# Reordering the start-up of a two-layer attention and mixture-of-experts kernel: which loads and clears stand ahead of the first slots

## The reference, cut to what matters

```python
x = x + tanh(g_xattn[0]) * attention(layernorm(x), ctx; 16 heads of 8, Wq Wk Wv Wo with biases)
x = x + tanh(g_ffn[0])   * experts(layernorm(x); 8 experts, hidden 256, each expert claims its best 512 tokens)
x = x + tanh(g_xattn[1]) * attention(layernorm(x), ctx; 16 heads of 8, no biases, no output matrix)
x = x + tanh(g_ffn[1])   * experts(layernorm(x); 8 experts, hidden 512, the best 2 of each token)
```

## Time and profile before

| | |
|---|---|
| runs (3) | 758.35, 759.71, 764.55 us; median 759.71 us |
| the profiled execution | 760.45 us, of which the trace spans 758.6 us |
| busy share of the span | PE 71%, PEld 57%, DVE 66%, ACT 47%, POOL 42% |
| chain that ended last | PE 41%, DVE 22%, issue 11%, POOL 10%, DMA 8%, ACT 5% |
| mean granted clock of PE | 0.869 |

### The profile page before, as it was taken

How to read it: one execution, slowest core, us unless ns; L and a number is a source line. 1 busy time by engine, 2 the same in 40 slices (tenths; PEclk the granted TensorE clock), 3 DMA queues, 4 the chain that set the end, 5 groups by cost and what they waited for, 6 DMA issues and landing times.

```text
span 758.6 us, 16969 instructions
## 1 busy us (share of the span) xinstructions
PE 539.6 (71%) x5534; PEld 435.7 (57%) x5534; DVE 502.7 (66%) x1605; ACT 358.3 (47%) x830; POOL 315.0 (42%) x439
## 2 busy tenths in 40 slices
PE   0699999998721039872699988888403999999940
PEld 0466777776510028761466756665302999999940
DVE  5568888887358862222699999998561556655625
ACT  0246777776633014330167766677402555555510
POOL 6212222221200057743755227456772455555440
PEclk9959999999955558996599999999755999999985
DMA  8443334332000004362556546241123222222229
GB/s 262 153 136 92 101 109 115 107 88 66 16 14 1 0 21 97 99 84 66 146 163 185 163 135 190 84 121 53 40 64 101 61 69 71 79 72 72 65 70 296
DMA packets 100532, 74.50 MB, mean 98 GB/s; under 512 B 12928, under 2 KB 94592, under 8 KB 100160
## 3 DMA queue, kind: packets, MB, share of 16 engines
q1 hardware_dynamic: 92336, 55.17, 25.5%
q0 software_dynamic: 7040, 14.56, 7.6%
q10 hardware_dynamic: 1072, 3.70, 1.4%
HBM read 43.64 MB, written 31.39 MB: 99 GB/s over the span
## 4 chain that ended last, share of the span: by engine, by line
PE 41%; DVE 22%; issue 11%; POOL 10%; DMA 8%; ACT 5%; SPq 2%; ACTq 1%; POOLq 0%; DVEq 0%
PE bank L943 10%; PE bank L953 10%; DVE MX L1089 7%; PE bank L740 5%; POOL PT L582 5%; PE bank L766 4%; PE bank L887 4%; PE bank L754 3%; POOL dispatched L556 3%; DVE PT L1285 2%; DMA PT<-normed,LIST 2%; PE bank L842 1%; ACT XT_HL_WR L654 1%; DMA QS_N<-MH 1%; ACT OT L678 1%
## 5 line engine op out<-in xcount | busy, mean ns | idle before, releaser
L623 ACT ACTIVATE PT<-bank 128x512 f32<-128x512 f32 x256 | 151.8, 597 | 95.1 <-PE bank L754 93.9
L1089 DVE TENSOR_REDUCE MX<-bank 128x4 f32<-128x512 f32 x256 | 172.1, 681 | 25.9 <-PE bank L766 24.2
L766 PE MATMUL bank<-KS,QS_N 96*128 96x128 f16 x1024 | 104.5, 228 | 16.7 <-DVE MX L1089 8.7
L593 POOL DMA_INDIRECT returned<-PT,META_ROW x78 | 74.9, 961 | 84.6 <-DVE PT L1403 72.4
L953 PEld LDWEIGHTS bank<-WALL,HT 128*128 128x128 f32 x808 | 100.9, 194 | 5.1 <-issue 1.7
L953 PE MATMUL bank<-WALL,HT 128*128 x808 | 102.1, 278 | 0.6 <-issue 0.6
L943 PE MATMUL bank<-XGT,XT_HL_WR 128*128 128x256 f32 x404 | 101.9, 392 | 0.0
L766 PEld LDWEIGHTS bank<-KS,QS_N 96*128 96x128 f16 x1024 | 76.6, 103 | 43.4 <-DVE MX L1089 15.3
L754 PE MATMUL bank<-QS_N,KS 98*128 98x512 f16 x256 | 98.0, 388 | 1.8 <-DMA QS_N<-MH 1.6
L943 PEld LDWEIGHTS bank<-XGT,XT_HL_WR 128*128 128x128 f32 x404 | 75.0, 198 | 8.0
L556 POOL DMA_INDIRECT dispatched<-N,SLOT x64 | 64.3, 1004 | 30.0 <-issue 14.1
(11 more groups left out here) (210 smaller groups left out, 917.4 us busy)
## 6 DMA issues: line engine op xcount, KB each, us to landing
spread<-XT_HL_WR SPq DMA_DIRECT2D x96, 128.0 KB, 2.0
QS_N<-spread SPq DMA_DIRECT2D x128, 48.0 KB
KS<-spread SPq DMA_DIRECT2D x32, 192.0 KB
PT<-dispatched SPq DMA_DIRECT2D x39, 132.0 KB, 2.1
WALL<-in_w SPq DMA_DIRECT2D x8, 578.0 KB
CT<-in_ctx SPq DMA_DIRECT2D x32, 128.0 KB
returned<-PT SPq DMA_DIRECT2D x23, 128.0 KB, 2.2
WALL<-in_w ACTq DMA_DIRECT2D x1, 2048.0 KB, 8.5
```

What stands on the lines that cost most here:

```text
L593: pool.indirect_dma_start(ys[1][:, :], bass.IndirectOffsetOnAxis(ap=META_ROW[:, a.f, c:c + 1], axis=0), YS[:, a.f, c, :], None).then_inc(S ...
L623: nc.scalar.activation(PT[:, c, 4 * g:4 * g + 4, :].rearrange("p j q -> p (j q)"), ST[i % 2][:, :], ACT.Exp, scale=SCALE[layer]).then_inc( ...
L766: last = nc.tensor.matmul(MB[i % 2][:, j * P:(j + 1) * P], QS[0:96, m.r, J * g + j, c * P:(c + 1) * P], KS[0:96, m.r, g, c * P:(c + 1) * P ...
L1089: V.tensor_reduce(out=MX[:, m.u, 2 * J * g + c:2 * J * (g + 1):2], in_=MB[i % 2][:, :].rearrange("p (j k) -> p j k", j=J), op=ALU.max, axi ...
```

## The change

SP loads the first two batches of `x` ahead of everything, on a semaphore of their own, then only four loads on `loaded`: the identity columns of `CONST`, `WSQ` 0 to 3, `VEC` and `GATES`. The other six of the first eight batches and three rest loads (the other columns of `CONST`, `WG`, `WSQ` 4 to 6) are issued by SP at slot -3, ahead of the context of pair 1. ACT takes the tanh at once, issues the other 24 batches at slot -2 and `ROWS` and `WALL` at slot 1. POOL clears `EXPO` and one quarter of `QS` first, and the others at the entry of slots -3 and -2; `KS` and the last quarter at slot -1. Each entry waits for POOL's own bias addition of the slot before. DVE clears one quarter of `VA` at the entry of each of the slots -4 to -1, makes `BIAS` at slot -3 ahead of the statistics of pair 1, three small clears at slot 1, and the four casts when the expert layer begins. The waits are moved to match.

```diff
-        LOADS = 6
+        LOADS, REST = 4, 3
...
         @block.sync
         def _(sp):
-            loads = [(CONST[:, :], const_in),
-                     (X[:, 0:FIRST * D].rearrange("p (b d) -> p b d", b=FIRST), x_in[0:FIRST].rearrange("b p d -> p b d")),
-                     (WSQ[:, :, :], wsq_in), (GATES[:, :], gates_in), (WG[:, :, :], wg_in), (VEC[:, :], vec_in)]
+            load_x(0, 2, x_first)
+            loads = [(CONST[:, 0:P], const_in[:, 0:P]), (WSQ[:, 0:4, :], wsq_in[:, 0:4, :]), (VEC[:, :], vec_in), (GATES[:, :], gates_in)]
...
+            def rest_of_loads(p):
+                if p == -3:
+                    load_x(2, FIRST, x_second)
+                    rest = [(CONST[:, P:], const_in[:, P:]), (WG[:, :, :], wg_in), (WSQ[:, 4:7, :], wsq_in[:, 4:7, :])]
+                    for to, of in rest:
+                        sp.dma_start(to, of).then_inc(rest_loaded, 16)
+                padding(p)
...
-                    sp.wait_ge(set_pool, 6)
+                    if r.g < 4:
+                        sp.wait_ge(set_pool, (2, 3, 4, 6)[r.r])
...
-            nc.gpsimd.memset(KS[96:98, :, :, :], SHIFT).then_inc(set_pool, 1)
+            def queries(r):
+                nc.gpsimd.memset(QS_N2[0:96, 2 * r * H * P:2 * (r + 1) * H * P].bitcast(F32), 0.0).then_inc(set_pool, 1)
+            nc.gpsimd.memset(EXPO[:, :], -0.5).then_inc(set_pool, 1)
             pool.wait_ge(set_pool, 1)
+            queries(0)
             pool.wait_ge(set_pool, 2)
-            for r in range(4):
-                nc.gpsimd.memset(QS_N2[0:96, 2 * r * H * P:2 * (r + 1) * H * P].bitcast(F32), 0.0).then_inc(set_pool, 1)
-                pool.wait_ge(set_pool, r + 3)
-            pool.wait_ge(loaded, 16 * LOADS)
+            def clear(p):
+                if p in (-3, -2, -1):
+                    pool.wait_ge(x_bias, p + 4)
+                if p in (-3, -2):
+                    queries(p + 4)
+                    pool.wait_ge(set_pool, p + 6)
+                if p == -1:
+                    nc.gpsimd.memset(KS[96:98, :, :, :], SHIFT).then_inc(set_pool, 1)
+                    pool.wait_ge(set_pool, 5)
+                    queries(3)
+                    pool.wait_ge(set_pool, 6)
...
             act.wait_ge(loaded, 16 * LOADS)
-            act.dma_start(X[:, FIRST * D:].rearrange("p (b d) -> p b d", b=B - FIRST),
-                          x_in[FIRST:].rearrange("b p d -> p b d")).then_inc(x_loaded, 16)
-            act.dma_start(ROWS[:, :], rows_in).then_inc(experts_loaded, 16)
-            act.dma_start(WALL[:, 0:E * WCOLS[0]], w0_in).then_inc(experts_loaded, 16)
             nc.scalar.activation(GATES[:, :], GATES[:, :], ACT.Tanh).then_inc(act_own, 1)
+            def rest_of_loads(p):
+                if p == -2:
+                    act.dma_start(X[:, FIRST * D:].rearrange("p (b d) -> p b d", b=B - FIRST),
+                                  x_in[FIRST:].rearrange("b p d -> p b d")).then_inc(x_loaded, 16)
+                if p == 1:
+                    act.dma_start(ROWS[:, :], rows_in).then_inc(experts_loaded, 16)
+                    act.dma_start(WALL[:, 0:E * WCOLS[0]], w0_in).then_inc(experts_loaded, 16)
...
             pe.wait_ge(loaded, 16 * LOADS)
-            pe.wait_ge(set_dve, 8)
...
+            def set_up(p):
+                if p < 0:
+                    r = p + 4
+                    V.memset(VA[:, r, :, :, :], 0.0).then_inc(set_dve, 1)
+                    dve.wait_ge(set_dve, 2 * r + 1)
+                    heads = VA[:, r, :, :, :].rearrange("p c h w -> p (c h w)").rearrange("p (k e w) -> p k e w", e=4, w=2 * HD)
+                    V.memset(heads[:, :, 0:4:3, HD:HD + 1], 1.0).then_inc(set_dve, 1)
+                    dve.wait_ge(set_dve, 2 * r + 2)
+                if p == -4:
+                    dve.wait_ge(x_first, 16)
+                if p == -3:
+                    dve.wait_ge(loaded, 16 * LOADS)
+                    dve.wait_ge(act_own, 1)
+                    dve.wait_ge(bias_done, 1)
+                    link(V.tensor_tensor(out=VEC[:, 0:D], in0=PO[:, 0:D], in1=VEC[:, 0:D], op=ALU.add))
+                    V.tensor_scalar(out=BIAS[:, :], in0=VEC[:, 0:D], scalar1=GATES[:, 0:1], scalar2=None,
+                                    op0=ALU.mult).then_inc(bias_done, 1)
+                    dve.wait_ge(x_second, 16)
+                if p == 0:
+                    dve.wait_ge(x_loaded, 16)
+                if p == 1:
+                    V.memset(MASKG[:, 0, 0, :], 0.0).then_inc(set_dve, 1)
+                    V.memset(N[:, :, D:ROW], 0.0).then_inc(set_dve, 1)
+                    V.memset(RX[:, 0:1], 0.0).then_inc(set_dve, 1)
+                    dve.wait_ge(set_dve, 11)
+                    dve.wait_ge(rest_loaded, 16 * REST)
...
             def expert_layer(layer):
                 if layer == 0:
+                    casts()
                     probabilities(layer)
```

More of the change, by code:

```diff
@@ L382, in _, with load_x @@
         def _(sp):
[L383 to L386 removed]
+            def load_x(b0, b1, sem):
+                sp.dma_start(X[:, b0 * D:b1 * D].rearrange("p (b d) -> p b d", b=b1 - b0), x_in[b0:b1].rearrange("b p d -> p b d")).then_inc(sem, 16)
+            load_x(0, 2, x_first)
+            loads = [(CONST[:, 0:P], const_in[:, 0:P]), (WSQ[:, 0:4, :], wsq_in[:, 0:4, :]), (VEC[:, :], vec_in), (GATES[:, :], gates_in)]
+            assert len(loads) == LOADS and at["ident"] == (0, P)
             for to, of in loads:
                 sp.dma_start(to, of).then_inc(loaded, 16)
+            def rest_of_loads(p):
+                if p == -3:
+                    load_x(2, FIRST, x_second)
+                    rest = [(CONST[:, P:], const_in[:, P:]), (WG[:, :, :], wg_in), (WSQ[:, 4:7, :], wsq_in[:, 4:7, :])]
+                    assert len(rest) == REST
+                    for to, of in rest:
+                        sp.dma_start(to, of).then_inc(rest_loaded, 16)
+                padding(p)
             def padding(p):
@@ L476, in second_experts @@
                     sp.dma_start(N2[:, b, 0:D], y[:, b, :]).then_inc(YL[k], 16)
-            pair_slots(0, attention_slot, padding)
+            pair_slots(0, attention_slot, rest_of_loads)
             first_experts()
@@ L594, in second_experts @@
                                                 YS[:, a.f, c, :], None).then_inc(SC[a.f], 16)
-            pair_slots(0, attention_slot(0))
+            pair_slots(0, attention_slot(0), clear)
             first_experts()
@@ L727, in _ @@
             for layer in range(2):
-                pair_slots(layer, attention_slot(layer))
+                pair_slots(layer, attention_slot(layer), None if layer else rest_of_loads)
                 expert_layer(layer)
@@ L969, in _ @@
             link = chain.link
[L970 to L974, removed]
-            V.tensor_copy(BEFORE[:, :], const("before")).then_inc(set_dve, 1)
-            V.tensor_copy(ONES[:, :], const("ones")).then_inc(set_dve, 1)
@@ L977, in _ @@
-            V.tensor_copy(SAME[:, :], const("same_expert")).then_inc(set_dve, 1)
-            V.tensor_copy(SHARE[:, :], const("region_share")).then_inc(set_dve, 1)
-            V.memset(MASKG[:, 0, 0, :], 0.0).then_inc(set_dve, 1)
-            V.memset(N[:, :, D:ROW], 0.0).then_inc(set_dve, 1)
-            V.memset(RX[:, 0:1], 0.0).then_inc(set_dve, 1)
-            dve.wait_ge(set_dve, 9)
-            dve.wait_ge(act_own, 1)
-            dve.wait_ge(bias_done, 1)
-            link(V.tensor_tensor(out=VEC[:, 0:D], in0=PO[:, 0:D], in1=VEC[:, 0:D], op=ALU.add))
@@ L986, in _ @@
-            V.tensor_scalar(out=BIAS[:, :], in0=VEC[:, 0:D], scalar1=GATES[:, 0:1], scalar2=None,
-                            op0=ALU.mult).then_inc(bias_done, 1)
+            def set_up(p):
[24 more added lines that the diff above has]
+                    dve.wait_ge(rest_loaded, 16 * REST)
@@ L989, in stats, with casts @@
+            def casts():
+                V.tensor_copy(BEFORE[:, :], const("before")).then_inc(set_dve, 1)
+                V.tensor_copy(ONES[:, :], const("ones")).then_inc(set_dve, 1)
+                V.tensor_copy(SAME[:, :], const("same_expert")).then_inc(set_dve, 1)
+                V.tensor_copy(SHARE[:, :], const("region_share")).then_inc(set_dve, 1)
+                dve.wait_ge(set_dve, 15)
             def stats(pair, tmp, mv):
```

18 lines of the change are left out of this document (11 added, 7 removed).

## The result

The changed kernel takes 756.0 us (median of 20, 752.43 to 762.29) against 759.49 us (median of 20): ratio 0.9959, 95% interval 0.9942 to 0.9975, so 1.9 to 4.4 us faster. The prediction was 751.7, 8.0 us faster. The sign and the place were right, the size was more than double. 756.0 lies inside the range, 748.7 to 756.5, but outside the forecast's own, 750.5 to 754. The profiled execution after took 754.38 us, of which the trace spans 752.5; only three of the 20 were quicker, so the 6.1 us between the two spans overstate the change's effect.

A forecast was written before the change was run, and what follows sets the result against it. The prediction took a serial start (loads, ACT's issues and tanh, `VEC`) as the bound. 9.8 - 1.3 - 0.5 = 8.0 us off 760.45 gave 752.45, with the median 0.74 lower 751.7; range 748.7 to 756.5, forecast's own 750.5 to 754.

The forecast's parts named there:

- S: Moment pair 0's last read-back lands and slot -1 begins: 29.37 us before, 20.9 predicted, 8.5 early.
- ACT: At the start, ACT's three DMA issues leave, so the tanh is done at 6.7 us instead of 15.1.
- Casts: Four casts move to where DVE idles 5.07 us for the last logits; bounds 0 and 2.1 us, 0 taken.
- DVE's start, slot -3: Transposes at 6.1 us, not 18.48; low part ends at 12.9, not 22.67, with POOL's 1.85 clear on the path; 9.8 remain.
- Transfers beside it: ACT's 24 batches run beside the third write and first reads; bounds 0 and 5.0 us lost, 1.3 taken.
- Slot -1, slot 0: POOL's chain ends at 23.1 us, wanted at 24.1, so hidden; slot 0 unchanged, padding still ahead of `MH`.
- Slot 1: `ROWS` and `WALL` load beside pair 1's `MH`; bounds 0 and 3.9 us lost, 0.5 taken.
- The second rule: All engines' DMAs interleave on the same 16 DMA engines; taken strictly, the sum is 4.3 us, or 755.4.
- B: Rival: POOL or the queues bound the start, with contention and late `GATES`; 5.1 us early, 754.6; chance 0.14.
- C: Rival: in slot 1 `WALL` delays `MH` to slot start + 9.0 and keeps PE's clock down; slower, 762.5; chance 0.04.
- A: Rival: no contention and PE's clock rises sooner; at best 10.9 us early, 748.8, centre 750; chance 0.16.
- D: Rival: the reordering doesn't reach S, as six batches or pair 0's context land late; 757; chance 0.04.

The follow-up runs named there:

- clears_twice: pieces_late with the second quarter of `QS` cleared three times over at slot -3; 754.37 us against 760.73 for the kernel before, ratio 0.9910.
- clears_later_alone: The changed kernel with each of POOL's clears one slot later, loads as they are; 758.29 us against 761.0 for the kernel before, ratio 0.9958.
- clears_later: pieces_late with each of POOL's clears one slot later; 748.75 us against 760.73 for the kernel before, ratio 0.9839.
- tables_late: The changed kernel with `ROWS` and `WALL` issued at slot 16 instead of slot 1; 795.77 us against 801.98 for the kernel before, ratio 0.9925.
- x_in_pieces: The changed kernel with the 24 batches loaded in six pieces of four, two slots ahead of use; 795.14 us against 801.98 before, ratio 0.9917.
- pieces_late: The changed kernel with both load edits, those of x_in_pieces and tables_late; 751.02 us against 760.73 for the kernel before, ratio 0.9858.
- again: The changed kernel unaltered, run once more; 797.49 us against 801.98 for the kernel before on the same chip, ratio 0.9948.
- after: The changed kernel in its first measurement and trace; 756.0 us against 759.49 for the kernel before, ratio 0.9959.
- again_2: The changed kernel unaltered, for a third trace; 757.61 us against 761.0 for the kernel before, ratio 0.9961.
- padding_late: clears_later with SP's 1 MB of padding issued at slot 16 instead of slot 0; 748.43 us against 761.0 for the kernel before, ratio 0.9831.
- before_again: The kernel before, unaltered, for a second trace; 760.21 us against 761.0 for the kernel before, ratio 0.9994.
- before_tanh_first: The kernel before with one edit, ACT's tanh ahead of its three DMA issues; 759.44 us against 760.73 for the kernel before, ratio 0.9987.
- clear_in_gap: The changed kernel with POOL's clear of the second quarter of `QS` moved from slot -3 into slot -4; 797.4 us against 801.98 before, ratio 0.9951.

## Why the prediction was right or wrong

- **What bounds the start.** Right: serial, loads then ACT then `VEC`. clears_twice shows that S moves the whole, one for one.
- **Loads.** Right: 128 KB of `x` land 2.1 us after issue (2.3 taken), `GATES` at 5.3 (5.2).
- **ACT.** Right in effect. The tanh ended at 5.50 and not 6.7, since the table load now stands ahead of the wait, at 0.74. It bought little: DVE's clear of `VA` ran until 6.80, and `VEC` and `BIAS` ended at 7.45, 7.5 having been said.
- **Casts.** Right, 0 in the sum: 0.16 to 0.22 us each behind, in front of an idle time of 4.77 us. The lines of the grouped view of DVE after, 200 to 213 us, with the row that answers to the earlier trace rows:

```profile
L1038 DVE CAST SAME<-CONST 128x128 bf16<-128x128 f32 x1 | 0.2, 219 | 0.0
```

```profile
211.84 0.42 DVE L1241 TENSOR_REDUCE SM<-LG 128x32 f32<-128x256 f32 x1 [4.77 <-ACT LG L716]
```

- **DVE's start, slot -3.** Right: transposes at 5.91 (6.1), low part ended at 12.64 (12.9) behind pair 1's `XN`, POOL's clear at 8.31 in front of it. That this clear is worth 1.85 us was right only for a kernel whose write isn't held: 0 in clears_later_alone, 1.3 at S in clears_later.
- **Transfers beside it: the step that failed first.** I took 1.3 us out of bounds of 0 and 5.0. The third write took 5.04 instead of 1.94, 3.1 more. The size was off because the mechanism was: I took half of one queue's delay because "here it is two", and two queues were no relief. The load's packets went first for 2 us, then one for one with the writes' smaller ones. Net of a low part 0.3 us early and shorter reads, S came 7.3 us early in the mean of the traces and not 8.5.
- **Slot -1, slot 0.** POOL's chain ended at 22.7 and was hidden, as said. Slot 0 had its padding wait, 3.71 us. But slot -1 lasted 9.09 us in all three traces of the changed kernel, and 8.35 and 8.85 before. The sum had no term for that. In tables_late, where PE took half as long for its queries, it lasted 8.15.
- **Slot 1: the step that failed second.** I took 0.5 us out of bounds of 0 and 3.9; `MH` took 6.32 us and landed with the large load: 40.95 + 8.5 = 49.45, and 43.47 + 6.32 = 49.79. It cost 1.1 us in the slot by tables_late, and 4.0 by x_in_pieces against pieces_late. I had reasoned that PE arrives late at its lower level; that hid part of the wait, not nearly all.
- **The sum.** Means of three traces after against two before: 7.3 us ahead at S, 6.8 at slot 0, 7.0 at slot 1, 5.2 at slot 2. In the prediction's terms that is 9.8 - 2.5 for the transfers, 0.5 lost in slot -1, 0.2 won in slot 0, and 1.8 lost in slot 1. Between the medians it is 3.5. The second rule, which the prediction set beside its sum, gave 755.4, and 756.0 was measured. Its direction was right, but the closeness is luck: it booked 5.0 for the transfers, where 2.5 were lost, and nothing for slot -1, for more than 0.5 in slot 1, or for what is lost behind slot 2. I gave it a note and no chance of its own.
- **The rivals.** Two were nearer than the forecast. B's contention, "as in the padding row", was booked at 3.2 and measured 3.1 at the write, and its 5.1 us early is near the 5.2 of slot 2; its late `GATES` and a POOL chain on the path of slot -1 didn't happen. C's first step happened too: `MH` landed with `WALL`, 8.0 us into the slot where C said 9.0, and over 5 us after its issue. Its second didn't: PE's clock wasn't held down, and was 1.00 from 47 to 62 us. A and D didn't happen; a clear of DVE was never blocked by POOL's.
- **What stays open.** Between slot 2 and the end the three traces of the changed kernel differ. Windows of the end of the first layer, again first, the changed kernel's first trace second:

```profile
190.00:200.00 10.00, 7.93 (x88) 5.25 (x88) 2.00 (x7) 5.71 (x14) 1.35 (x4) 0.83 0.04 13
```

```profile
190.00:200.00 10.00, 8.35 (x130) 5.85 (x128) 2.19 (x8) 7.57 (x18) 1.35 (x4) 1.00 0.10 30
```

  With PE's granted clock at 0.83 it gets through 88 instructions instead of 130, and again loses 2.7 us in slot 15 that after and again_2 don't. What goes before it is the last `MH` load. The chain of again, and what moved between its issue and its landing (187.74 to 191.46); then the changed kernel's first trace from issue to landing (187.43 to 189.84):

```profile
188.29 3.17 DMA QS_N<-MH
```

```profile
q1 hardware_dynamic: 367, 0.15, 14.0%
q8 instruction: 1, 0.02, 1.6%
```

```profile
q1 hardware_dynamic: 96, 0.02, 3.5%
```

  In again a transfer of 16 KB of the kind "instruction" falls into that stretch, `MH` lands in 3.17 us instead of 1.86, and PE's next 32 products take 1.86 us instead of 1.01. In the other trace such a transfer comes at 190.77, after `MH`. The same holds over all fourteen traces. In six (again, clears_later_alone, pieces_late, clears_twice, clears_later, padding_late) it starts between issue and landing, the second `MH` issue takes 3.2 to 3.8 us, and slot 15 lasts 9.5 to 11.7 us. In the other eight it comes after the landing, the issue takes 1.8 to 1.9, and slot 15 lasts 7.9. That is a coincidence without exception, not an experiment: no run moved that transfer. It hit none of the traces of before, before_again and before_tanh_first, and six of the eleven with the changed start. Whether an earlier start makes it likelier, and whether it is the whole of the 1 to 2 us by which the changed kernel's medians fall short of its 5.2, stays open. Of clears_later, whose trace lost 6 us there, the traced execution took 755.2 us and the five others 748.0 to 750.2, so most executions seem to be spared.

## What to carry to other kernels

When a start is reordered, the loads taken out of its way must go somewhere, and "later, on another engine's queue" is not a place off the path: put no transfer of megabytes in flight just before a small one that an engine waits for. Cut it into pieces that land before the next small transfer, or issue it where nothing small is due; here that turned 3.5 us of gain into some 10, and 12 with POOL's clears a slot later. Read the packets of both queues before saying how one transfer holds another: landings alone look the same when it stands still and when it shares. And split a gain at an early mark by slots before giving it to an edit; part of it may be a slot in which PE happened to run faster. And where the profile shows work hidden behind a wait (the casts behind the tanh), ask what is late once that wait goes, since it is the next bound.

## What the runs showed of the hardware

- **A small transfer issued on SP's queue 2 to 4.5 us after a large one on ACT's landed 0.2 to 0.4 us after the large one.** Third write against the 24 batches (landing, from issue and time to landing, good to 0.05): 17.70 against 17.3 (after), 17.71 and 17.3 (again), 17.49 and 17.1 (again_2), 18.33 and 18.0 (clear_in_gap), 17.84 and 17.6 (clears_later_alone), 17.73 and 17.4 (tables_late). `MH`, 8 KB, against `WALL`: 49.79 and 49.45, 49.55 and 49.33, 49.46 and 49.13, 50.35 and 50.15, 49.85 and 49.52, 47.01 and 46.82 (x_in_pieces). The packets show two ways to this. Beside packets of 2 KB the writes' packets of 0.5 KB first moved not at all (1 against 148 from 10 to 12 us), then one for one (396 against 417 from 12.5 to 15.5). Beside packets of 16 KB no small packet moved for 3 us (0 against 70 from 43 to 46). The Trainium skill, "DMA: Bandwidth & Descriptors", section Issuing engines are not separate DMA queues, says that DMAs of all engines end on the same 16 DMA engines and interleave. The trace agrees for the writes; for `MH` beside `WALL` no interleaving is seen in those 3 us.
- **One instruction transfer of 16 KB (q8) between issue and landing went with an 8 KB load of 3.2 to 3.8 us instead of 1.8 to 1.9**, in six traces of fourteen, without exception either way (see above).
- **DVE's `XN`, a tensor_scalar from SBUF to SBUF, ran 1.87 us instead of 0.60 beside a clear of POOL's**, ending 0.15 us after it. Other operations of DVE kept their lengths beside such a clear: in the changed kernel L1011 (a clear) took 0.91 us both at 5.71, alone, and at 12.79, inside POOL's clear of 12.71 to 14.51, and the statistics at 13.92, inside it too, took 0.29 as ever. "SBUF — State Buffer", section Who interferes with whom, in the Trainium skill, names tensor_scalar among those that can take the port pair that DVE shares with GpSimd; the trace agrees for `XN`.
- **ACT's table load went ahead of the wait where the tanh is ACT's first work**: at 0.74 us in the changed kernel and in before_tanh_first, against 13.61 before, behind the issues.
